# A gated recurrence: outputs moved to GpSimd, products left in PSUM, seven row places

## The chip, the cores and the metric

The kernel runs on one core of a Trainium2 chip. The metric is the time on the device in microseconds from the first to the last instruction with what lies around it, the median of the runs; lower is better. The core has a matrix engine (TensorE, "PE"), which writes to PSUM only; a vector engine (VectorE, "DVE"); an engine for activations (ScalarE, "ACT"); and GpSimd ("POOL"), which works on SBUF. Each follows its own queue in order and waits on semaphores.

## The reference, cut to what matters

One decoder layer on x of shape (2, 1024, 256): gated linear attention, a cross attention over 64 gathered context rows, and a block with self attention and 8 experts, a layer norm behind each. The change touches the first one alone:

```
q, k: (2, 1024, 16 heads, 8);  v: (2, 1024, 16, 16)
g = log_sigmoid(x @ Wgk1 @ Wgk2 + bgk2) / 16
h[t] = h[t-1] * exp(g[t])[..., None] + k[t][..., None] * v[t][..., None, :]   # scan over t
o[t] = einsum('bhk,bhkv->bhv', q[t] * 8**-0.5, h[t])
o = o * rsqrt(mean(o*o) + eps) * gnw * silu(x @ Wg);  x = layernorm(x + o @ Wo)
```

## The kernel before

The function `front` holds the whole of the first attention. The 128 partitions are 16 heads times 8 key channels; the free axis is the 1024 tokens of one batch. The 16 value columns of 2 batches make NJ = 32 steps jj. A step works on one row of 1024 values per partition:

- `values(jj)` on PE: 4 matmuls with a selection matrix spread value column jj over the key channels, into PSUM banks 2 (jj % 2) and the next, so two steps have places.
- `product(jj)` on DVE (L521): those banks times KT (the keys), into place jj % 6 of the SBUF tile `qh`.
- `state(jj)` on DVE (L526): the scan h = decay * h + product, in place in `qh`.
- `output(jj)` on DVE (L531): `qh` times QT (the queries), in place.
- `sums(q)` on PE (L314), for four steps at a time: matmuls with `headsum` add the 8 key channels of each head; then ACT copies the result (`OT`, L686), PE transposes it (`turn`, L320), ACT puts it into the token rows O (`tokens`, L689).

The semaphores s_v, s_kv, s_h, s_qh and s_s count the values, products, scans, outputs and sums that are done. `values(jj)` waits for product jj-2 (`s_kv`), and `product(jj)` for the sums that free its place of `qh`. On DVE the loop reads: scan jj; the extra work of this step if it is one of a first kind; product jj+1; output jj; the extra work if it is of a second kind.

The order of each queue is written out by hand. Extra work lies at fixed steps. Of the first kind on DVE: the rounding remainders of the value parts `parts_lo` (steps 2, 12, 19; L514) and of x `x_lo` (steps 4, 6; L505), `log_sigmoid` (11), `out_means` of block 0 (18), `out_rstd` (23, 28), which ends in the small operation called `nmr`. Of the second kind: `out_gated` (19, 21; L846 to L850, the result is the tile z), `out_means` of block 1 (20), `out_stats` (22, 27; L134 and L139), the key and value blocks of the cross attention (30; L602). On PE in step jj: `values(jj+2)`, then every fourth step `sums` and `turn`, in others the projections of the second batch, the gates, the transposes of z (19 and 25), the output products (L866 and L867; 21, 22, 26, 27), the matmuls of the context's keys (29, 30; L458 to L465), and `counts`, one-hot matmuls of the token lists. ACT makes the one-hot rows for them with 65 sign operations (`signs`, L696), spread over the steps, besides all the copies out of PSUM that are not on DVE. After the last step the ends of all these lead into the next block of the program, which PE, DVE and ACT enter together.

GpSimd sets constants and issues DMAs until 22 us, and then does nothing until the next block.

Of the kernel before, what the change touches and what calls it, by code (L numbers as in the profile page):

```python
# [16 lines left out]
ALU = mybir.AluOpType  # L17
# [44 lines left out]
class Kernel:  # L62
# [99 lines left out]
    def front(self, c):  # L162
# [8 lines left out]
        RQ, RS = 6, 6  # L171
# [52 lines left out]
        PASSES = ((0, 0), (1, 0), (0, 1))  # L224
        with nc.Block() as block:
# [10 lines left out]
            def _(e):  # L236
# [14 lines left out]
                for h in range(P // HD):  # L251
                    e.dma_start(gnw[h * HD:(h + 1) * HD, :], a["L0_attn_gnw"].rearrange("(p o) -> p o", o=1)).then_inc(s_wo, 16)
            @block.tensor
            def _(e):
# [41 lines left out]
                def values(jj):  # L296
                    n, j = jj // DK, jj % DK
                    if jj >= 2:
                        e.wait_ge(s_kv, jj - 1)
                    elif jj:  # L300
                        e.wait_ge(V.sem, V.at("k0"))
                    else:
                        e.wait_ge(self.C.sem, self.C.at(f"sel{DK - 1}"))
# [174 lines left out]
                e.wait_ge(s_kv, NJ)  # L478
# [15 lines left out]
            def _(e):  # L494
# [20 lines left out]
                def product(jj):  # L515
                    e.wait_ge(s_v, jj + 1)
                    if jj == HD:
                        e.wait_ge(A.sem, A.at("k1"))
                    if jj >= RQ:
                        e.wait_ge(s_s, (jj - RQ) // 4 + 1)  # L520
                    e.tensor_tensor(qh[:, jj % RQ, :], wide(2 * (jj % 2)), KT[:, batch(jj // HD)], ALU.mult).then_inc(s_kv, 1)  # L521
                def state(jj):
                    e.wait_ge(s_kv, jj + 1)
                    if jj % HD == 0:
                        e.wait_ge(A.sem, A.at(f"decay{jj // HD}"))
                    e.tensor_tensor_scan(qh[:, jj % RQ, :], decay[:, batch(jj // HD)], qh[:, jj % RQ, :], 0.0, ALU.mult, ALU.add).then_inc(s_h, 1)  # L526
                def output(jj):
                    e.wait_ge(s_h, jj + 1)
                    if jj % HD == 0:
                        e.wait_ge(A.sem, A.at(f"q{jj // HD}"))  # L530
                    e.tensor_tensor(qh[:, jj % RQ, :], qh[:, jj % RQ, :], QT[:, batch(jj // HD)], ALU.mult).then_inc(s_qh, 1)  # L531
# [32 lines left out]
                for jj in range(NJ):  # L564
                    state(jj)
                    if jj == 2:
# [17 lines left out]
                    if jj + 1 < NJ:  # L584
                        product(jj + 1)
                    output(jj)
# [2223 lines left out]
```

## Time and profile before

| | us |
|---|---|
| median of 3 runs (lowest, highest) | 1365.08 (1364.91, 1366.44) |
| the profiled execution: span of its instructions | 1364.6 |
| DVE busy in the whole span | 984.8 (72%) |
| PE busy in the whole span | 1288.8 (94%) |
| 32 scans, busy | 73.0 |
| 32 products, busy | 38.6 |
| 32 outputs, busy | 38.9 |
| 65 sign operations of ACT, busy | 70.7 |
| recurrence on DVE, first product to last output | 23.3 to 194.3 |

A row of a timeline is: start in us, duration in us, engine, line, operation, output tile <- input tiles, shapes, and in brackets the idle time of the engine just before it with what ended it. A duration runs from an instruction's start to its end; the next one of the same engine can start about 0.1 us before that end. A list of waits names the engine and line that waited, what it waited for, the sum in us, the number of times and the longest. A table of stretches gives for each engine the busy us and the instructions, and PEclk, the clock granted to TensorE as a share of 2.4 GHz; it is 0.5 at the engine's lower level of 1.2 GHz.

### The profile page before, as it was taken

How to read it: one execution, taken by the hardware profiler on the slowest of the kernel's cores; microseconds unless marked ns; L12 is line 12 of the kernel's file. 1: busy time of each engine (PE TensorE's matmuls, PEld its weight loads, DVE VectorE, ACT ScalarE, POOL GpSimd, SP SyncE). 2: the span in 40 equal slices, each digit the busy share in tenths (PEclk: the TensorE clock that was granted, in tenths of full speed). 3: DMA queues.
4: the chain of work that ended last, by engine and by line, in shares of the span. 5: the costliest groups of instructions: out<-in, count | busy, mean ns of one | idle time of the engine just before them, and what ended most of it. 6: DMA issues, size and time to landing. Idle time of an engine off the chain costs nothing.

```text
span 1364.6 us, 19112 instructions
## 1 busy us (share of the span) xinstructions
PE 1288.8 (94%) x7622; PEld 953.5 (70%) x7622; DVE 984.8 (72%) x1417; ACT 642.7 (47%) x942; POOL 139.4 (10%) x220
## 2 busy tenths in 40 slices
PE   8786868999899999999999999999999999999997
PEld 6453536667655555558888788888888888888886
DVE  7999997898799888848676655655646555555566
ACT  5787664346468877874433432322223223223233
POOL 5000003000524433310000000000000000000000
PEclk9898889999999999989999999999999999999999
DMA  5000001003612212203000011201101102010001
GB/s 140 1 1 0 0 1 35 1 1 133 200 49 70 60 52 55 59 29 109 16 1 16 16 55 41 72 21 39 47 9 47 39 16 70 16 39 16 0 16 47
DMA packets 40328, 55.78 MB, mean 41 GB/s; under 512 B 9552, under 2 KB 26624, under 8 KB 40240
## 3 DMA queue, kind: packets, MB, share of 16 engines
q1 hardware_dynamic: 35056, 43.67, 10.7%
q0 software_dynamic: 3648, 10.09, 2.5%
q8 instruction: 60, 0.98, 0.3%
q10 hardware_dynamic: 1536, 0.81, 0.2%
q14 instruction: 28, 0.23, 0.1%
HBM read 43.73 MB, written 10.55 MB: 40 GB/s over the span
## 4 chain that ended last, share of the span: by engine, by line
PE 52%; DVE 2%; ACT 0%; issue 0%; ACTq 0%; DVEq 0%
PE PS L2502 25%; PE PS L2515 24%; PE PS L2265 1%; PE PS L114 0%; PE PS L2528 0%; PE PS L2246 0%; PE PS L2279 0%; DVE OT_all L2663 0%; DVE r_st L2341 0%; DVE r_on L2358 0%; DVE r_on L2338 0%; PE PS L2540 0%; DVE X L2350 0%; DVE x_mid L2654 0%; ACT X L2624 0%
## 5 line engine op out<-in xcount | busy, mean ns | idle before, releaser
L2585 ACT ACTIVATE x_g<-PS,x_bias 128x512 f32<-128x512 f32 x256 | 175.8, 687 | 493.0 <-PE PS L2502 492.9
L2502 PE MATMUL PS<-x_h,x_w 128*128 128x512 f32 x1536 | 398.6, 395 | 0.0
L2515 PE MATMUL PS<-x_mid,x_w 128*128 128x512 f32 x1488 | 383.9, 393 | 1.1 <-DVE x_w L2237 1.1
L2502 PEld LDWEIGHTS PS<-x_h,x_w 128*128 128x128 f32 x1536 | 285.9, 188 | 64.7
L2515 PEld LDWEIGHTS PS<-x_mid,x_w 128*128 128x128 f32 x1488 | 279.6, 188 | 65.6 <-DVE x_w L2237 1.6
L2654 DVE CAST x_mid<-x_g 128x512 fp32r<-128x512 f32 x256 | 109.3, 427 | 268.0 <-ACT x_g L2585 267.7
L2104 DVE TENSOR_REDUCE a_M<-PS 128x2 f32<-128x1024 f32 (+1 forms) x144 | 173.1, 1223 | 24.6 <-PE PS L1801 18.5
L2656 DVE TENSOR_TENSOR x_mid<-x_g,x_mid 128x512 fp32r<-128x512 f32 x256 | 177.2, 692 | 8.8
L2042 ACT ACTIVATE f_parts<-PS 128x512 f32<-128x512 f32 x224 | 120.7, 601 | 36.5 <-PE PS L1855 24.9
L1878 PE MATMUL PS<-f_parts,aV 128*32 128x256 f32 (+1 forms) x960 | 75.1, 394 | 0.2 <-POOL f_parts L1689 0.2
L526 DVE TENSOR_TENSOR_SCAN qh<-decay,qh 128x1024 f32<-128x1024 f32 x32 | 73.0, 2282 | 0.0
L696 ACT ACTIVATE c_hot<-c_idxT,c_cid 128x1024 bf16<-128x1024 bf16 x65 | 70.7, 1140 | 3.5 <-PE PS L337 2.2
L2482 POOL DMA_DIRECT2D x_wb<-route_w x31 | 16.7, 539 | 476.3 <-DVE OT_all L2663 453.4
L1855 PE MATMUL PS<-aQ,aK 64*128 64x512 f32 x192 | 50.7, 485 | 0.5 <-ACT f_h L2042 0.5
L2663 DVE SCALAR_TENSOR_TENSOR OT_all<-PS,x_bias,x_wb 128x512 f32<-128x512 f32 x62 | 46.2, 745 | 0.0
L1855 PEld LDWEIGHTS PS<-aQ,aK 64*128 64x128 f32 x192 | 20.3, 183 | 37.0 <-ACT f_parts L2042 27.0
L1689 POOL TENSOR_SCALAR_AFFINE_SELECT f_parts<-f_parts 128x512 f32<-128x512 f32 x45 | 28.5, 634 | 162.2 <-ACT f_parts L2042 142.7
L307 PE MATMUL PS<-vparts,g_sel 128*128 128x512 f32 x128 | 39.3, 432 | 5.2 <-DVE qh L521 4.5
L1797 PE MATMUL PS<-aK,aQ 64*128 64x512 f32 (+3 forms) x256 | 36.3, 327 | 7.0 <-PEq L1058 2.7
L2237 DVE TENSOR_TENSOR x_w<-x_raw,x_w 128x1024 fp32r<-128x1024 f32 x32 | 39.4, 1233 | 2.0 <-ACT x_w L2232 2.0
L521 DVE TENSOR_TENSOR qh<-PS,KT 128x1024 f32<-128x1024 f32 x32 | 38.6, 1206 | 1.4 <-PE PS L314 1.3
L531 DVE TENSOR_TENSOR qh<-qh,QT 128x1024 f32<-128x1024 f32 x32 | 38.9, 1215 | 0.0
(383 smaller groups left out, 1593.9 us busy)
## 6 DMA issues: line engine op xcount, KB each, us to landing
x_raw<-L_ffn_e_w SPq DMA_DIRECT2D x32, 512.0 KB, 3.8
qk_parts<-f_parts SPq DMA_DIRECT2D x16, 512.0 KB, 3.3
x_wb<-route_w POOLq DMA_DIRECT2D x31, 256.0 KB, 3.4
aQ<-qk_parts SPq DMA_DIRECT2D x96, 64.0 KB, 2.5
aK<-qk_parts SPq DMA_DIRECT2D x60, 64.0 KB, 2.7
X<-x SPq DMA_DIRECT2D x4, 512.0 KB, 7.5
aK<-qk_parts SPq DMA_DIRECT2D x36, 48.0 KB, 2.0
out<-X SPq DMA_DIRECT2D x3, 512.0 KB, 2.9
```

The source lines that it names most:

```text
L526: e.tensor_tensor_scan(qh[:, jj % RQ, :], decay[:, batch(jj // HD)], qh[:, jj % RQ, :], 0.0, ALU.mult, ALU.add).then_inc(s_h, 1)
L696: e.activation(hot[:, n % RS, :], self.idxT[:, :], ACT.Sign, bias=self.cid[:, c:c + 1], scale=2.0).then_inc(s_sg, 1)
L1855: last = e.matmul(bank, K[q][R, s, tile(TB * h if kind == "k0" else kind)], Q[q][R, s, q0:q0 + BLK], start=True, stop=True)
L1878: last = e.matmul(PS[32 * j:32 * j + 32, 7, dst:dst + w], Vs[m % 2][:, kt, j, :], x, start=k in (0, 3) and half == 0, stop=k in (2, NQD - ...
L2042: e.activation(buf[k][:, j, :], PS[:, 4 + b % 3, :], ACT.Exp).then_inc(A.sem, 1)
L2104: e.tensor_reduce(dst, src, AX.X, ALU.max, negate=True).then_inc(VC.sem, 1)
L2502: last = e.matmul(PS[:, f % 2, :], w1[n % 2][u][:, kt, f * P:(f + 1) * P], self.rows(v, k)[:, kt, :], start=m == 0 and kt == 0, stop=m == ...
L2515: last = e.matmul(PS[:, 2 + 2 * (it % 2) + d, :], w2[n % 2][v][:, f, d * P:(d + 1) * P], mid[u][:, f % RM, :], start=f == 0 and m == 0, st ...
L2585: e.activation(g[s % RG][:, :], PS[:, f % 2, :], ACT.Gelu, bias=b1[:, n, f:f + 1]).then_inc(A.sem, 1)
L2654: e.tensor_copy(mid[0][:, f % RM, :], g[s % RG][:, :]).then_inc(V.sem, 1)
L2656: e.tensor_tensor(mid[1][:, f % RM, :], g[s % RG][:, :], mid[0][:, f % RM, :].bitcast(F32), ALU.subtract).then_inc(V.sem, 1)
L2663: e.scalar_tensor_tensor(out=(y if n else sumT[k])[:, d, :], in0=PS[:, 2 + 2 * (it % 2) + d, :], scalar=b2[:, n, d:d + 1], in1=wb[:, it % ...
```

## The change

GpSimd takes the outputs of steps 0 to 30, in order, behind its constants; the last one stays on DVE. The product is written back into the PSUM banks in which the values stand, and the scan reads it there and writes to `qh`. So `values(jj)` waits for scan jj-2 in place of product jj-2, and the wait for a free place of `qh` moves from the product to the scan. `qh` has seven places instead of six. On DVE product jj+1 now follows scan jj directly, ahead of the extra work of both kinds. At the end of the queue PE's transposes of x, which overwrite bank 0, wait for 31 scans instead of 32 products.

```diff
-        RQ, RS = 6, 6
+        RQ, RS = 7, 6
...
             @block.gpsimd
...
+                for jj in range(NJ - 1):
+                    output(e, jj)
...
                 def values(jj):
...
-                        e.wait_ge(s_kv, jj - 1)
+                        e.wait_ge(s_h, jj - 1)
...
-                e.wait_ge(s_kv, NJ)
+                e.wait_ge(s_h, NJ - 1)
                 self.c_turn(e, 0)
...
-                    if jj >= RQ:
-                        e.wait_ge(s_s, (jj - RQ) // 4 + 1)
-                    e.tensor_tensor(qh[:, jj % RQ, :], wide(2 * (jj % 2)), KT[:, batch(jj // HD)], ALU.mult).then_inc(s_kv, 1)
+                    e.tensor_tensor(wide(2 * (jj % 2)), wide(2 * (jj % 2)), KT[:, batch(jj // HD)], ALU.mult).then_inc(s_kv, 1)
                 def state(jj):
                     e.wait_ge(s_kv, jj + 1)
                     if jj % HD == 0:
                         e.wait_ge(A.sem, A.at(f"decay{jj // HD}"))
-                    e.tensor_tensor_scan(qh[:, jj % RQ, :], decay[:, batch(jj // HD)], qh[:, jj % RQ, :], 0.0, ALU.mult, ALU.add).then_inc(s_h, 1)
-                def output(jj):
...
+                    if jj >= RQ:
+                        e.wait_ge(s_s, (jj - RQ) // 4 + 1)
+                    e.tensor_tensor_scan(qh[:, jj % RQ, :], decay[:, batch(jj // HD)], wide(2 * (jj % 2)), 0.0, ALU.mult, ALU.add).then_inc(s_h, 1)
...
                 for jj in range(NJ):
                     state(jj)
+                    if jj + 1 < NJ:
+                        product(jj + 1)
+                    else:
+                        output(e, jj)
                     if jj == 2:
                         parts_lo(1)
...
-                    if jj + 1 < NJ:
-                        product(jj + 1)
-                    output(jj)
                     if jj == 19:
                         self.out_gated(e, 0)
```

## Rows read from the trace of the kernel before

**Rows 1.** Busy time by stretch: us, PE, PEld, DVE, ACT, POOL, PEclk, DMA share, GB/s

```profile
124.00:147.00 23.00, 16.35 (x92) 10.72 (x96) 22.86 (x20) 14.95 (x16) 0.00 (x0) 0.85 0.00 1
```

**Rows 2.** Timeline of DVE: output, scan and product of neighbouring steps

```profile
108.09 1.21 DVE L531 TENSOR_TENSOR qh<-qh,QT 128x1024 f32<-128x1024 f32 x1
109.22 2.28 DVE L526 TENSOR_TENSOR_SCAN qh<-decay,qh 128x1024 f32<-128x1024 f32 x1
111.43 1.20 DVE L521 TENSOR_TENSOR qh<-PS,KT 128x1024 f32<-128x1024 f32 x1
```

**Rows 3.** Timeline of DVE: the first product and the first scan

```profile
23.31 1.22 DVE L521 TENSOR_TENSOR qh<-PS,KT 128x1024 f32<-128x1024 f32 x1
24.57 2.29 DVE L526 TENSOR_TENSOR_SCAN qh<-decay,qh 128x1024 f32<-128x1024 f32 x1
```

**Rows 4.** Waits of DVE, 24 to 195 us: sum in us, times, longest

```profile
DVE XTp L505 <- ACT XTp L651: 2.6, 1, 2.6
DVE qh L521 <- PE PS L314: 1.3, 1, 1.3
DVE vparts L514 <- ACT vparts L681: 1.3, 2, 0.9
```

**Rows 5.** Waits of PE for DVE, 59.5 to 122 us

```profile
PE PS L263 <- DVE XTp L505: 1.4, 1, 1.4
PE PS L314 <- DVE vparts L514: 0.7, 1, 0.7
```

**Rows 6.** Timeline of DVE: `parts_lo` of step 19, the gating of block 0, scan 20

```profile
122.64 1.23 DVE L514 TENSOR_TENSOR vparts<-PS,vparts 128x1024 fp32r<-128x1024 f32 x1 [0.92 <-ACT vparts L681]
...
126.04 0.55 DVE L846 RECIPROCAL go_rs<-go_rs 128x64 f32<-128x64 f32 x1
...
129.02 2.28 DVE L526 TENSOR_TENSOR_SCAN qh<-decay,qh 128x1024 f32<-128x1024 f32 x1
```

**Rows 7.** Timeline of ACT: the square roots of blocks 0 and 1

```profile
123.92 0.35 ACT L841 ACTIVATE go_rs<-go_ms,eps 128x64 f32<-128x64 f32 x1
...
138.68 0.31 ACT L841 ACTIVATE go_rs<-go_ms,eps 128x64 f32<-128x64 f32 x1
```

**Rows 8.** Timeline of PE, 129 to 198 us

```profile
129.25 1.94 PE L114 MATMUL PS<-ident,z 128*128 128x128 f32 x8 [6.77 <-DVE z L850]
...
142.27 1.20 PE L307 MATMUL PS<-vparts,g_sel 128*128 128x512 f32 x4
...
145.46 0.59 PE L867 MATMUL PS<-X,ident 128*128 128x256 f32 x2
...
152.05 2.07 PE L307 MATMUL PS<-vparts,g_sel 128*128 128x512 f32 x4 [4.52 <-DVE qh L521]
...
177.24 3.62 PE L314 MATMUL PS<-qh,headsum 128*32 128x512 f32 x16 [5.60 <-ACT X L886]
...
186.42 1.03 PE L465 MATMUL PS<-decay,c_L 128*128 128x256 f32 x4
...
195.56 1.92 PE L314 MATMUL PS<-qh,headsum 128*32 128x512 f32 x16
```

**Rows 9.** Timeline of DVE: statistics of blocks 0 and 1, key blocks, scan 31

```profile
146.47 1.42 DVE L134 BATCH_NORM_STATS2 go_st<-PS 128x6 f32<-128x256 f32 x4
...
170.84 1.42 DVE L134 BATCH_NORM_STATS2 go_st<-PS 128x6 f32<-128x256 f32 x4
...
187.73 2.48 DVE L602 TENSOR_TENSOR c_Kblk<-PS,c_m 128x512 f32<-128x512 f32 x4
...
190.79 2.28 DVE L526 TENSOR_TENSOR_SCAN qh<-decay,qh 128x1024 f32<-128x1024 f32 x1
```

**Rows 10.** Timeline of POOL, 11 to 18 us

```profile
11.78 1.16 POOL L943 TENSOR_SCALAR_AFFINE_SELECT c_selaug<-c_selaug 128x1024 fp32r<-128x1024 f32 x1
...
13.77 2.84 POOL L943 TENSOR_SCALAR_AFFINE_SELECT c_selaug<-c_selaug 128x256 fp32r<-128x256 f32 x3
17.11 0.42 POOL L943 TENSOR_SCALAR_AFFINE_SELECT c_selaug<-c_selaug 128x256 fp32r<-128x256 f32 x1 [0.50 <-POOL c_selaug L943]
```

More of the change, by code:

```diff
@@ L224, in front, with output @@
         PASSES = ((0, 0), (1, 0), (0, 1))
+        def output(e, jj):
+            e.wait_ge(s_h, jj + 1)
+            if jj % HD == 0:
+                e.wait_ge(A.sem, A.at(f"q{jj // HD}"))
+            e.tensor_tensor(qh[:, jj % RQ, :], qh[:, jj % RQ, :], QT[:, batch(jj // HD)], ALU.mult).then_inc(s_qh, 1)
         with nc.Block() as block:
@@ L525, in state @@
                         e.wait_ge(A.sem, A.at(f"decay{jj // HD}"))
-                    e.tensor_tensor_scan(qh[:, jj % RQ, :], decay[:, batch(jj // HD)], qh[:, jj % RQ, :], 0.0, ALU.mult, ALU.add).then_inc(s_h, 1)
-                def output(jj):
[L528 to L531, printed above, removed]
+                    if jj >= RQ:
+                        e.wait_ge(s_s, (jj - RQ) // 4 + 1)
+                    e.tensor_tensor_scan(qh[:, jj % RQ, :], decay[:, batch(jj // HD)], wide(2 * (jj % 2)), 0.0, ALU.mult, ALU.add).then_inc(s_h, 1)
                 e.wait_ge(A.sem, A.at("wl"))
```

## The prediction

> **What bounds the kernel now.** I read the busy time by stretch first, since the change touches only the recurrence (23 to 194 us of the profiled execution). There DVE is busy nearly all the time, 22.86 of 23 us in the stretch from 124, PE and ACT much less [rows 1]. Next its own order: a step is scan, product, output, and the starts lie 1.13 us apart from output to scan and 2.21 from scan to product; with 1.11 from product to output (1.20 long, less the overlap of 0.09 that the output shows too) a step is 4.45 us [rows 2]. A scan that follows its own product directly, as the first one does, starts 1.26 us after it, so 0.13 later than one with work in between [rows 3]. So taking 31 outputs from DVE looks like 31 x 1.13 = 35.0 us. But the list of what DVE waited for has three entries in the recurrence: x_lo 2.6, a product 1.3, parts_lo 1.3 (two times) [rows 4]. They are short, and they are the places to look at: at each, DVE had caught up with a chain on PE and ACT, and a faster DVE only waits longer there. What PE waited for between 59.5 and 122 us settles it: on DVE only 1.4 us once and 0.7 us once, each right behind one of those same two DVE operations [rows 5]. Between them PE and ACT ran at their own pace. The reader should see two lists with almost equal lengths, not one busy engine and two idle ones.
>
> **Part 1, up to the gating of block 0: about 2 us gained.** The x_lo of step 6, the parts_lo of step 12 and the parts_lo of step 19 each ended an idle time of DVE, behind ACT copies that hang on PE. They can't start earlier, so the 6, 12 and 19 outputs ahead of them buy nothing. What is gained is what stood between the joint and the next scan: the product moves ahead of it and the output goes. At the third joint parts_lo starts at 122.64 and gating at 126.04 [rows 6]; two operations go, 1.11 + 1.13 us [rows 2], but gating then meets ACT's square root, which ended at 124.27 and, by my estimate, ends 0.3 earlier now [rows 7]. I put gating at 124.0, scan 20 at 127.0 instead of 129.02, 2.0 earlier. The seventh row place is costed at nothing here: the buffer wait behind it is the 1.3 us product wait of rows 4 late in the recurrence, and the waits of part 2 lie over it.
>
> **Part 2, the new hand-over.** Before, the selection matmuls of step j+2 (`values`) waited for product j; now they wait for scan j, since the scan reads the bank. From then DVE has product j+1 and scan j+1, 1.26 + 2.20 = 3.5 us, until it wants product j+2. Queued behind this wait on PE is everything of step j+2 and later: sums, transposes, output products. PE's matmuls for one step take 1.20 us and the sums of four steps 1.92 [rows 8], so two or three steps in four carry more than 3.5 us of PE work, and the rest waits. Leg by leg, with the durations of before:
> - From the transposes of z (129.25) through ACT to the square root of block 1 (138.68) 9.43 us pass on PE and ACT [rows 7, 8]. From 127.25 that gives 136.7, its end 137.0. Gating takes 129.02 - 126.04 = 2.98 [rows 6], scan 22 runs from 140.0 to 142.3, and only then may `values(24)` go. From its start (142.27) to the end of the output product behind it (145.46 + 0.59) are 3.8 us [rows 8]: 146.1. The statistics of block 0 start at 146.2 instead of 146.47 [rows 9]. The 2 us are down to 0.3.
> - From the statistics to scan 23 I take 1.9 us, 1.42 for their first part [rows 9] and an estimate of 0.4 for the small second. Scan 23 starts at 148.05, scan 24 2.20 + 1.26 later at 151.5, ends at 153.8; `values(26)` starts at 153.85, where before it started at 152.05, behind product 24 [rows 8]. Now 1.8 us late.
> - From `values(26)` to the statistics of block 1 (170.84) 18.8 us pass on PE with waits on ACT alone [rows 8, 9]: 172.65, 1.8 late.
> - From there to the sums of group 6 (177.24) 6.4 us pass over the statistics, scan 28, the small `nmr` operation, ACT's row copies [rows 8, 9]. Product 29 now stands ahead of `nmr`, 1.13 more: 180.2, 2.95 late.
> - PE and ACT take it from there to the matmuls of the keys (186.42 + 1.03 = 187.45) [rows 8], now 190.4. The key blocks on DVE started at 187.73 [rows 9], 0.28 after; now at once, 190.4. So they, scan 31 (190.79 before, 193.5 now) and all behind them are **2.7 us later**.
>
> **Part 3, what the clock gives back.** The granted clock was 0.85 in the stretch from 124 us [rows 1]: PE fell to its 1.2 GHz level in the long waits (6.77, 4.52 and 5.60 us), and the matmuls right behind them ran at it. At that level `values` took 2.07 instead of 1.20 us, the sums 3.62 instead of 1.92 [rows 8], so a low spell that catches both costs 2.6 us, and two of them (152 and 177 us) 5.1. The new order splits these gaps: the one ahead of `values(26)` is cut by `values(25)`, the one ahead of the sums by `values(30)`. If they vanish, the sum is 2.7 - 5.1 = -2.4; if a third one is added, by the new wait of `values(24)`, 2.7 + 2.6 = +5.3. I take a relief of 1.0, since a gap of over 4 us stays ahead of `values(25)` (146.1 to 150.4) and of `values(30)`. Sum: +2.7 - 1.0 = **+1.7 us**.
>
> **Operations the trace doesn't show.** A product that writes PSUM, and a scan that reads it: the nearest rows are a PSUM-read product at 1.20 us and an SBUF-only output at 1.22 [rows 2]. Bounds: 0.1 faster to 1.2 slower (a second pass). Only two products and three scans lie on the path above, so -0.2 to +3; DVE's new slack (31 us of idle) hides the others. I take 0, nearest in kind. The output on GpSimd: the nearest row is a one-input operation of the same size, 1.16 us [rows 10]; a second input makes 1.2 to 2.3. Next to DVE work the same small operation took 2.84/3 = 0.95 us instead of 0.42 [rows 10], so the upper bound is 2.3 x 2.25 = 5.2 us. I take 2.3. The new mean step is (193.5 - 24.6)/31 = 5.4 us, and a group's sums come behind a `values` that waits for the next scan, so anything up to 5.2 us is covered and costs nothing. GpSimd's queue is free by 23 us; its next work stands in the next block. That cover is gone above 5.4 us. The last output stays on DVE, 1.2 us as before.
>
> The long pieces of 0.95 us lay beside DVE operations on SBUF operands. The Trainium skill (SBUF — State Buffer, "Who interferes with whom") says a DVE instruction with two SBUF inputs contends with a GpSimd instruction that reads SBUF, one with a single SBUF input doesn't; the trace of before agrees as far as those rows go and can't show the second half. The skill's GPSIMD Engine Reference (section 3.1) also speaks against moving two-input work there, about 2.6 cycles per element; at its 1.2 GHz an estimate from that page is 2.2 us, and the sum would be the same.
>
> **The rivals.**
> A. DVE alone is the bound and PE keeps up: -31 x 1.13 - 1.3 + 32 x 0.13 = -32 us, 1333. For it: DVE's busy share [rows 1]. Against: rows 4 and 5. Chance 0.05. A weaker form, in which the late legs are loose and only the joints of part 1 hold, gives back the 11 outputs after scan 20, -2 - 11 x 1.13, less 3 = about -11, 1354: 0.10.
> B. The legs hold, and PE stays at 2.4 GHz because its gaps are split: -2.4, 1362.7. Chance 0.17, half of it faster than the bound.
> C. The legs hold, and the wait of `values(24)` and `values(25)` adds a low spell: +5.3, 1370.4. Chance 0.13. Slower side; it decides once PE idles in front of step 22 as long as it did ahead of the slow matmuls of rows 8.
> D. GpSimd becomes the bound: from 5.4 us per output on. At 6 us the last of 31 ends at 26.9 + 186 = 213, and the last sums, at 195.6 before [rows 8], wait for it: +17, 1382. It needs the SBUF contention also with the scans. Chance 0.05. A product of twice the length, with DVE as the bound again, about 1372: 0.02.
> Forecast, legs as worked out, clock about as before: 0.48.
>
> **How the numbers follow.** The span of 1364.6 us lies 0.5 below the median of 1365.08; the sum is a difference and goes onto the median: 1365.1 + 1.7 = 1366.8. What a measurement can tell from no change is 0.2%, 2.7 us: faster is under 1362.4, slower above 1367.8. The forecast's own spread (1.5 us either way, ACT's 65 one-hot operations shifting against PE) puts two thirds of 0.48 inside, a third above. Faster: 0.15 + 0.08 = 0.23. Same: 0.31 + 0.09 = 0.40. Slower: 0.17 + 0.13 + 0.07 = 0.37. The range leaves out both forms of A, D and the double product, 0.22 in all: 1359 to 1371.5. The forecast's own range is 1363 to 1370.
>
> **What the profile after would show.** DVE's busy time in the recurrence 31 outputs (37.8 us) lower while its end hardly moves; DVE idle ahead of products, released by the `values` matmuls, of x_lo and parts_lo, and of the statistics, released by the output products, some 30 us in all. x_lo still at 58 to 59 us, parts_lo at 88 and 122 to 123. PE waiting on scans ahead of `values(24)` to `values(26)`. Scans and products within 0.1 us of before. GpSimd at 2 to 2.5 us an output, mostly idle. Wrong if DVE shows no such waits (A), if PE waits for GpSimd (D), or if the statistics of block 1 start before 168 us: then leg 3 fails.

## The result and the profile after

| | before | after |
|---|---|---|
| median of 19 runs each on one chip (lowest, highest), us | 1365.4 (1363.7, 1369.2) | 1368.64 (1364.9, 1370.9) |
| ratio after to before, 95% interval | | 1.0019 [1.0012, 1.0026] |
| span of the profiled execution, us | 1364.6 | 1367.8 |
| DVE busy in the whole span, us | 984.8 | 955.3 |

The change takes 31 outputs from DVE, and the kernel is slower by 0.19%, 2.6 us by the ratio (3.2 by the medians). The interval excludes no change, but the loss is only about the 0.2% that the prediction took as the least that a measurement can tell. The runs of one kernel spread over some 6 us (1364.9 to 1370.9 for after), and each kernel has one trace, of one execution: after's took 0.9 us more than its median. So verdicts go by medians and ratios, and traces are read for where the time goes.

The costliest groups of the page of after that the change touches (line, engine, operation, tiles, shapes, count | busy us, mean ns | idle before, releaser):

```profile
L229 POOL TENSOR_TENSOR qh<-qh,QT 128x1024 f32<-128x1024 f32 x31 | 73.7, 2377 | 89.5 <-DVE qh L534 89.5
L534 DVE TENSOR_TENSOR_SCAN qh<-decay,PS 128x1024 f32<-128x1024 f32 x32 | 73.0, 2281 | 0.6
L527 DVE TENSOR_TENSOR PS<-PS,KT 128x1024 f32<-128x1024 f32 x32 | 38.9, 1217 | 18.4 <-PE PS L315 18.3
```

All three unknown operations are as costed: an output on GpSimd takes 2.38 us (2.3 taken), and the product and scan over PSUM last as long as in [rows 2]. GpSimd waits for a scan ahead of every output, and no engine's list of waits names it. The scans wait 0.6 us in all, so the seventh place of `qh` is enough; it was not priced alone. Now DVE's list of waits, 24 to 195 us, which answers [rows 4]:

```profile
DVE PS L527 <- PE PS L315: 18.3, 11, 5.3
DVE go_st L134 <- PE PS L871: 8.3, 2, 5.5
DVE XTp L513 <- ACT XTp L655: 3.1, 2, 2.6
DVE vparts L522 <- ACT vparts L685: 2.4, 3, 1.6
DVE go_rs L850 <- ACT go_rs L845: 2.2, 2, 1.8
```

5.2 us of waits have become 38 (with three small ones not shown, 3.5 us together): the freed time has turned into waiting for PE's `values` (L315), for the output products (L871) and for ACT. The end of the recurrence didn't come nearer. Leg by leg, from the two timelines (start in us):

| | before | after, forecast | after, measured | difference |
|---|---|---|---|---|
| `x_lo` of step 6 | 58.59 | not earlier | 55.60 | -3.0 |
| scan 20 | 129.02 | 127.0 | 124.15 | -4.9 |
| scan 22 | 142.03 | 140.0 | 137.69 | -4.3 |
| statistics of block 0 | 146.47 | 146.2 | 143.84 | -2.6 |
| scan 24 | 153.05 | 151.5 | 150.35 | -2.7 |
| `values(26)` | 152.05 | 153.85 | 152.68 | +0.6 |
| statistics of block 1 | 170.84 | 172.65 | 171.01 | +0.2 |
| sums of group 6 | 177.24 | 180.2 | 179.61 | +2.4 |
| key blocks on DVE | 187.73 | 190.4 | 191.22 | +3.5 |
| scan 31 | 190.79 | 193.5 | 194.29 | +3.5 |

PE after, 124 to 191 us, which answers [rows 8]: the new waits are the ones released by `DVE qh L534`, the scans.

```profile
124.38 1.94 PE L114 MATMUL PS<-ident,z 128*128 128x128 f32 x8 [5.06 <-DVE z L854]
...
140.02 1.19 PE L315 MATMUL PS<-vparts,g_sel 128*128 128x512 f32 x4 [2.01 <-DVE qh L534]
...
143.21 0.59 PE L871 MATMUL PS<-X,ident 128*128 128x256 f32 x2
148.01 2.07 PE L315 MATMUL PS<-vparts,g_sel 128*128 128x512 f32 x4 [4.21 <-DVE qh L534]
...
152.68 2.08 PE L315 MATMUL PS<-vparts,g_sel 128*128 128x512 f32 x4 [1.62 <-DVE qh L534]
...
175.18 2.07 PE L315 MATMUL PS<-vparts,g_sel 128*128 128x512 f32 x4 [4.21 <-DVE qh L534]
179.61 3.64 PE L322 MATMUL PS<-qh,headsum 128*32 128x512 f32 x16 [2.36 <-ACT X L890]
184.40 1.97 PE L328 MATMUL PS<-ident,OT 128*128 128x128 f32 x8 [1.15 <-ACT OT L690]
```

`values(24)` waits 2.01 us for scan 22, and the output products that stand behind it on PE, which the statistics of block 0 need, wait with it. The statistics are at 143.84, when 143.21 + 0.59 has ended. DVE had nothing to do from 141.1 on. In all PE waits 12.3 us for scans in the recurrence, in five places.

One row was not foreseen. The small operation `nmr`, 0.16 us before, in both blocks (DVE, then GpSimd, then ACT after):

```profile
175.04 1.21 DVE L527 TENSOR_TENSOR PS<-PS,KT 128x1024 f32<-128x1024 f32 x1
176.16 0.17 DVE L148 RECIPROCAL go_rstd<-go_sd 128x4 f32<-128x4 f32 x1
176.36 1.23 DVE L884 SCALAR_TENSOR_TENSOR go_nmr<-go_mv,go_rstd 128x4 f32<-128x4 f32 x1
```

```profile
175.20 2.36 POOL L229 TENSOR_TENSOR qh<-qh,QT 128x1024 f32<-128x1024 f32 x1 [8.41 <-DVE qh L534]
```

```profile
177.62 1.93 ACT L890 ACTIVATE X<-PS,go_nmr,go_rstd 128x256 f32<-128x256 f32 x4 [2.26 <-DVE go_nmr L884]
```

`nmr` works on 4 values per partition and ends at 177.59, just when GpSimd's output ends (175.20 + 2.36 = 177.56). The row copies and the sums of group 6 stand behind it.

### The profile page after: what moved, and what is told of

It reads as the page before. It is cut to its first block, busy times and chain, and to the rows that moved or that the text cites. A ratio compares the mean times of both kernels' runs of the same rounds, so it can differ in the third digit from the quotient of the medians.

```text
span 1367.8 us, 19111 instructions
## 1 busy us (share of the span) xinstructions
PE 1290.3 (94%) x7622; PEld 953.9 (70%) x7622; DVE 955.3 (70%) x1386; ACT 642.9 (47%) x942; POOL 213.7 (16%) x251
## 4 chain that ended last, share of the span: by engine, by line
PE 52%; DVE 2%; ACT 0%; issue 0%; ACTq 0%; DVEq 0%
PE PS L2506 25%; PE PS L2519 24%; PE PS L2269 1%; PE PS L114 0%; PE PS L2532 0%; PE PS L2250 0%; PE PS L2283 0%; DVE OT_all L2667 0%; DVE r_st L2345 0%; DVE r_on L2362 0%; DVE r_on L2342 0%; PE PS L2544 0%; DVE X L2354 0%; DVE x_mid L2658 0%; ACT X L2628 0%
## 5 line engine op out<-in xcount | busy, mean ns | idle before, releaser
L229 POOL TENSOR_TENSOR qh<-qh,QT 128x1024 f32<-128x1024 f32 x31 | 73.7, 2377 | 89.5 <-DVE qh L534 89.5
L534 DVE TENSOR_TENSOR_SCAN qh<-decay,PS 128x1024 f32<-128x1024 f32 x32 | 73.0, 2281 | 0.6
L315 PE MATMUL PS<-vparts,g_sel 128*128 128x512 f32 x128 | 41.8, 453 | 13.1 <-DVE qh L534 12.3
L527 DVE TENSOR_TENSOR PS<-PS,KT 128x1024 f32<-128x1024 f32 x32 | 38.9, 1217 | 18.4 <-PE PS L315 18.3
L315 PEld LDWEIGHTS PS<-vparts,g_sel 128*128 128x128 f32 x128 | 24.4, 210 | 26.4 <-DVE qh L534 16.6
```

## Experiments

All ratios are to the kernel before on the same chip at the same time, 95% intervals in brackets. Kernels of different times are compared by their ratios; 0.1% is 1.37 us. The places in us are from one traced execution each, and these lie differently to their medians: those of `a_gwait`, `a_nmr1`, `a_noout` and `b_noout` took 3.2, 2.6, 1.9 and 1.2 us less than the median, those of `a_order2` and `b_order` 2.8 and 1.0 more. The kernel after and `a_gwait` do the same work up to scan 19 and start that scan at 115.60 and 113.92 us.

### Outputs left out of the kernel before, and of the kernel after

Both leave out 31 output products (so the sums add the states, not the states times the queries). `b_noout` keeps the old hand-over, `a_noout` the new one.

```diff
 b_noout
-                    output(jj)
+                    if jj == NJ - 1:
+                        output(jj)
 a_noout
-                for jj in range(NJ - 1):
-                    output(e, jj)
 both
-                    e.wait_ge(s_qh, 4 * q + 4)
+                    e.wait_ge(s_h, 4 * q + 4)
+                    if q == NQ - 1:
+                        e.wait_ge(s_qh, 1)
```

> The kernel before, with the 31 outputs of steps 0 to 30 left out on every engine (the sums read the states themselves); product, hand-over and order as before. It asks what DVE's 35.0 us of outputs are worth without the new wait. Two-lists theory (PE and ACT bind at the joints): 3 to 7 us faster than before, about 1360.5; x_lo, parts_lo still wait for ACT, parts_lo of step 19 at 119 to 121 us; values(26) at about 147.5, as it still waits for a product. DVE-is-the-bound rival: 30 to 35 us faster, about 1332, no new idle time on DVE.

> The kernel after, with its 31 outputs on GpSimd left out (the sums read the states); product in PSUM and the new hand-over kept. Two-lists theory: GpSimd is not on the path but for the two small nmr operations that read two SBUF operands (1.23 us instead of 0.16), so 2 us faster than after, about 1366.5, and about as slow as before. GpSimd rival (the outputs on GpSimd slow DVE or delay the sums): 5 us or more faster than after, 1363 or less.

`b_noout`: 1362.9 us, 0.9986 [0.9976, 0.9995], less than the 3 to 7 us of the theory; the rival (30 to 35) is far off. This is what taking the outputs off DVE brings in this order with nothing put in their place: 1.9 us of the 35 that stood on DVE. In the trace scan 20 is at 124.22, 4.8 earlier than before, and the key blocks at 182.91, still 4.8 earlier. So the whole gain comes by scan 20, as in after, and 3.0 of it stand at the `x_lo` of step 6 already (55.58 against 58.59); the later outputs buy nothing.

`a_noout`: 1365.4 us, 1.0006 [0.9996, 1.0016], 1.8 us by the ratio ahead of after, as the theory had it. Scan 20 at 122.42, the key blocks at 186.34. From scan 20 on it loses 5.2 us against `b_noout` (63.92 against 58.69 us): the new hand-over, together with the new order on DVE, which the two kernels also differ in. Over the whole, by the ratios, it is 2.7 us. The operation `nmr` is short again without GpSimd beside it:

```profile
147.40 0.17 DVE L148 RECIPROCAL go_rstd<-go_sd 128x4 f32<-128x4 f32 x1
147.60 0.16 DVE L884 SCALAR_TENSOR_TENSOR go_nmr<-go_mv,go_rstd 128x4 f32<-128x4 f32 x1
```

### One SBUF input for nmr

The mean is left out: `nmr` is minus the root alone, so that it reads one SBUF tile instead of two.

```diff
+        if m < 2:
+            e.tensor_scalar(self.o_nmr[m % 2][:, :], self.o_rstd[m % 2][:, :], -1.0, None, ALU.mult).then_inc(self.OV[m].sem, 1)
+            return
```

> The kernel after, with the two nmr operations of blocks 0 and 1 in a form with one SBUF tensor input (the mean is left out of them, so these blocks' normalisation lacks it). Port theory (a DVE operation with two SBUF inputs waits until GpSimd's running output ends): nmr at 0.15 to 0.2 us instead of 1.23, both on the path, 2 us faster, 1366.5. Rival (nmr is long because it follows the reciprocal or the product closely): nmr stays at 1.2 us and the time at 1368.6.

1368.9 us, 1.0028 [1.0017, 1.0039]: nothing gained, and the row says why.

```profile
173.54 1.21 DVE L527 TENSOR_TENSOR PS<-PS,KT 128x1024 f32<-128x1024 f32 x1
174.65 0.17 DVE L148 RECIPROCAL go_rstd<-go_sd 128x4 f32<-128x4 f32 x1
174.85 1.23 DVE L885 TENSOR_SCALAR go_nmr<-go_rstd 128x4 f32<-128x4 f32 x1
```

GpSimd's output ran from 173.70 to 176.07, `nmr` ended at 176.08: it waited as before. The numbers are the rival's, but its cause is not: in `a_noout` (above) and `a_gwait` (below) `nmr` follows the reciprocal just as closely, without GpSimd beside it, and takes 0.16. A theory that counts inputs alone is wrong, and the prediction gave the page's rule without its condition when it wrote that an instruction with a single SBUF input doesn't contend. The reciprocal beside it, one SBUF input too, did not wait (0.17). The Trainium skill (SBUF — State Buffer, "Who interferes with whom") has the missing half: besides instructions with two SBUF inputs, a `tensor_scalar` from SBUF to SBUF can take the shared pair of ports in one of its two-port modes. The trace agrees: 1.23 us, ended with GpSimd's output to 0.01. No run here has this `tensor_scalar` without GpSimd beside it (the form with two inputs takes 0.16 then), and why the reciprocal stays out no run here tests.

### GpSimd held back at two steps

```diff
                 for jj in range(NJ - 1):
+                    if jj == 23:
+                        e.wait_ge(self.OV[0].sem, self.OV[0].at("nmr"))
+                    elif jj == 28:
+                        e.wait_ge(self.OV[1].sem, self.OV[1].at("nmr"))
                     output(e, jj)
```

> The kernel after, where GpSimd starts the outputs of steps 23 and 28 only once the small operation nmr of block 0 and of block 1 has ended; nothing else differs, nothing is left out. Theory: nmr took 1.23 instead of 0.16 us because it wants the SBUF port that GpSimd holds for its output; with GpSimd held back nmr is 0.16 again in both blocks, the row copies and the sums of group 6 are 1.1 us earlier, and the ratio to before falls from 1.0019 by 0.001 to 0.002, to 1.000 to 1.001; the two outputs start about 0.3 to 0.5 us later than before and nobody waits for them. It is read from the medians and from nmr's row. Rival (GpSimd's price in the medians, 3 us against the kernel with its outputs left out, is not these two waits but the clock or other waits): nmr shortens and the ratio stays at 1.0015 to 1.0025.

1366.4 us, 1.0010 [0.9999, 1.0020]. It falls by 0.0009, about the least that the theory had, and the interval overlaps that of after, so the verdict rests on the trace. DVE and then GpSimd:

```profile
174.23 0.16 DVE L888 SCALAR_TENSOR_TENSOR go_nmr<-go_mv,go_rstd 128x4 f32<-128x4 f32 x1
```

```profile
174.48 4.67 POOL L229 TENSOR_TENSOR qh<-qh,QT 128x1024 f32<-128x1024 f32 x2 [9.78 <-DVE go_nmr L888]
```

From the statistics of block 1 to the sums of group 6 pass 176.42 - 168.88 = 7.54 us, against 8.60 in after: 1.06 less, the length of the port wait. (My fourth leg had 6.40 + 1.13 = 7.53.) The kernel is level with `a_noout` (1.0010 and 1.0006, each to 0.001), so nothing of a price of GpSimd is left that these runs can measure.

### The old hand-over with GpSimd, and the new one with DVE's outputs

`a_sbuf` is the kernel after with the product in SBUF again and `values` behind the product. `b_psum` is the kernel before with the product left in PSUM, `values` behind the scan and seven places of `qh`. In both the wait for a free place moves along, to the operation that writes `qh` first (cut from the lines below). Nothing is left out of either.

```diff
 a_sbuf
-                        e.wait_ge(s_h, jj - 1)
+                        e.wait_ge(s_kv, jj - 1)
...
-                    e.tensor_tensor(wide(2 * (jj % 2)), wide(2 * (jj % 2)), KT[:, batch(jj // HD)], ALU.mult).then_inc(s_kv, 1)
+                    e.tensor_tensor(qh[:, jj % RQ, :], wide(2 * (jj % 2)), KT[:, batch(jj // HD)], ALU.mult).then_inc(s_kv, 1)
...
-                    e.tensor_tensor_scan(qh[:, jj % RQ, :], decay[:, batch(jj // HD)], wide(2 * (jj % 2)), 0.0, ALU.mult, ALU.add).then_inc(s_h, 1)
+                    e.tensor_tensor_scan(qh[:, jj % RQ, :], decay[:, batch(jj // HD)], qh[:, jj % RQ, :], 0.0, ALU.mult, ALU.add).then_inc(s_h, 1)
 b_psum
-        RQ, RS = 6, 6
+        RQ, RS = 7, 6
...
-                        e.wait_ge(s_kv, jj - 1)
+                        e.wait_ge(s_h, jj - 1)
...
-                    e.tensor_tensor(qh[:, jj % RQ, :], wide(2 * (jj % 2)), KT[:, batch(jj // HD)], ALU.mult).then_inc(s_kv, 1)
+                    e.tensor_tensor(wide(2 * (jj % 2)), wide(2 * (jj % 2)), KT[:, batch(jj // HD)], ALU.mult).then_inc(s_kv, 1)
...
-                    e.tensor_tensor_scan(qh[:, jj % RQ, :], decay[:, batch(jj // HD)], qh[:, jj % RQ, :], 0.0, ALU.mult, ALU.add).then_inc(s_h, 1)
+                    e.tensor_tensor_scan(qh[:, jj % RQ, :], decay[:, batch(jj // HD)], wide(2 * (jj % 2)), 0.0, ALU.mult, ALU.add).then_inc(s_h, 1)
```

> The kernel after with the product written to SBUF (qh) as before and the old hand-over (values waits for the product), outputs on GpSimd. Port theory: the scan now has two SBUF inputs and waits for GpSimd's output of the step before, so a step is 2.4 + 2.3 + 0.1 = 4.8 us where nothing else waits, scan rows of 3 us and more, and the whole is 3 to 10 us slower than before, about 1372. Rival (no contention, the new hand-over alone cost the gain): scans stay 2.28 us and the time is that of the kernel before without outputs, 4 to 5 us faster than before, about 1361.

> The kernel before with the product left in PSUM, the scan reading it there, `values` behind scan j-2 and seven row places; all 32 outputs stay on DVE, in the old order. Nothing is left out. It prices the new hand-over with the old DVE load. With 31 outputs left out, the new hand-over together with the new order cost 2.4 us in the medians (1362.9 against 1365.4), since a `values` behind scan j then has 3.5 us of DVE work to hide in. Theory (the wait costs what DVE's queue no longer covers): here an output of 1.1 us stands in that stretch too, 4.6 us, so the PE work of most steps fits and `values` is late only at steps with sums; ratio to before 1.000 to 1.0015, PE waiting on scans ahead of the same `values` (25 and 26) for 2 to 4 us. Rival (the hand-over costs a fixed 3.5 us or more wherever it stands, through the low-clock matmuls that its waits bring): 1.0025 or above. Second rival (the seventh place and the free wait ahead of the scan instead of the product matter): below 0.999.

`a_sbuf`: 1369.5 us, 1.0029 [1.0017, 1.0041], 4.0 us slower than before by the ratio, within the theory's 3 to 10; the rival (faster than before) fell. Its scans, first the group and then two of them with the product between:

```profile
L534 DVE TENSOR_TENSOR_SCAN qh<-decay,qh 128x1024 f32<-128x1024 f32 x32 | 92.9, 2903 | 0.6
```

```profile
94.90 3.43 DVE L534 TENSOR_TENSOR_SCAN qh<-decay,qh 128x1024 f32<-128x1024 f32 x1
98.25 1.19 DVE L529 TENSOR_TENSOR qh<-PS,KT 128x1024 f32<-128x1024 f32 x1
99.48 3.48 DVE L534 TENSOR_TENSOR_SCAN qh<-decay,qh 128x1024 f32<-128x1024 f32 x1
```

17 of 32 scans take 3.3 to 3.5 us instead of 2.28. The output on GpSimd starts when a scan ends (98.41), the product has no second SBUF input and runs beside it in 1.19 us, the next scan (decay and `qh`, both SBUF) starts at 99.48 and ends 2.15 us after the output's end at 100.81. So it stands still until GpSimd has finished. A plain step is 99.48 - 94.90 = 4.58 us; with the outputs on DVE it was 4.45. Here the rule can be laid beside rows: the Trainium skill (SBUF — State Buffer, "Who interferes with whom") says that a DVE instruction with two SBUF inputs contends with a GpSimd instruction that reads SBUF, and one with a single SBUF input outside the two-port modes doesn't; the trace agrees, after has 2.28 us for a scan that reads its product from PSUM, `a_sbuf` 3.48. So leaving the product in PSUM is what keeps the scans short beside GpSimd. It doesn't pay for the new hand-over, though: after is only 0.0010 ahead of `a_sbuf`, 1.4 us, and the two intervals overlap.

`b_psum`: 1372.0 us, 1.0053 [1.0040, 1.0067]. The theory (0 to 0.15%) fell, its rival held. PE's waits for scans in this kernel, and the place where output products stand behind one:

```profile
PE PS L307 <- DVE qh L526: 19.9, 12, 4.2
```

```profile
148.58 1.20 PE L307 MATMUL PS<-vparts,g_sel 128*128 128x512 f32 x4 [2.01 <-DVE qh L526]
...
151.78 0.59 PE L867 MATMUL PS<-X,ident 128*128 128x256 f32 x2
156.58 2.08 PE L307 MATMUL PS<-vparts,g_sel 128*128 128x512 f32 x4 [4.21 <-DVE qh L526]
```

The statistics of block 0 start at 152.41, 5.9 us later than before, those of block 1 at 179.36, 8.5 later; the key blocks at 195.73, 8.0 later. My error was to look at the free time behind a step's `values`. What counts is what `values` now holds up on PE. From scan 20 on that is the output products with the statistics behind them. But scan 20 itself is at 132.99, 4.0 later than before: half of the loss arises where PE's waits hold up gates, sums and projections (7.7 of the 19.9 us lie before 128 us). That DVE, still full, can make up for nothing afterwards fits both halves, but no run tests it. So the hand-over alone costs 7.2 us by the ratio; with the outputs gone and the new order on DVE, 2.7 (`a_noout` against `b_noout`). The outputs alone bring 1.9. The two parts don't add: 7.2 - 1.9 = 5.3 us, and both together measured 0.8 (`a_noout`).

### The order behind the new wait

`a_pe` puts PE's output products ahead of the `values` of their step. `a_order2` has this, `out_rstd` ahead of the product as in the kernel before, and GpSimd held back as above. `b_order` is the kernel before with PE's move alone. Nothing is left out. The lines taken out at the old places, and those that hold GpSimd back, are cut here.

```diff
                 for jj in range(NJ):
+                    if jj == 22:
+                        self.out_product(e, 0, SB, (2, 3))
+                    elif jj == 27:
+                        self.out_product(e, 1, SB, (2, 3))
                     if jj + 2 < NJ:
                         values(jj + 2)
...
                     state(jj)
+                    if jj == 23:
+                        self.out_rstd(e, 0)
+                    elif jj == 28:
+                        self.out_rstd(e, 1)
                     if jj + 1 < NJ:
                         product(jj + 1)
```

> The kernel after with three places reordered, nothing left out: PE's output products of token tiles 2 and 3 of both blocks (steps 22 and 27) stand ahead of the `values` of their step instead of behind it, `out_rstd` with nmr stands ahead of the product again, as in the kernel before, and GpSimd holds back the outputs 23 and 28 until nmr has ended. Theory (the new wait costs because the output products are queued behind it on PE, and the statistics, the root and the sums of group 6 hang on them): the statistics of block 0 start at 141.1 instead of 143.8 in the profiled execution, those of block 1 about 4 us earlier than 171.0, the sums of group 6 5 to 6 us earlier than 179.6, and the whole is 3 to 6 us faster than the kernel after, ratio to before 0.9975 to 0.9995. Rival (the legs are set by the scans of DVE, or what is gained is lost in later waits at the keys and the last sums): statistics earlier, the start of scan 31 less than 1.5 us earlier, and a ratio of 1.001 to 1.002.

> The kernel before with the same move on PE alone: the output products of tiles 2 and 3 of both blocks ahead of the `values` of their step. Nothing is left out. Before, this `values` waited for nothing there, so the move buys only its length, 1.2 us at each of two places, and product 24 (or 29) may come later by 2.6 us, which DVE's queue (scan 23 and the root in between) hides. Theory: 0.5 to 2 us faster, ratio 0.9985 to 0.9997, so less than the same move brings the kernel after; if so, the changed kernel with it is about level with or ahead of this one. Rival (the order of PE is worth as much here, 3 to 6 us): 0.9955 to 0.998, and the change then is not what should be kept.

> The kernel after with PE's move alone: output products of tiles 2 and 3 of both blocks ahead of the `values` of their step; `out_rstd` stays behind the product and GpSimd holds nothing back. Nothing is left out. It divides the 5.9 us between the kernel with only GpSimd held back (1366.4) and the one with all three moves (1360.5). Theory (the queue position of the output products behind the new wait is the main cost): statistics at 141 and 167 us, nmr 1.23 us in both blocks, and 1363.0 to 1364.5, ratio 0.9985 to 0.9998; the order of `out_rstd` and the port wait are then worth 2.5 to 4 us together. Rival (the gain comes from `out_rstd` ahead of the product): 1365.5 or more, ratio above 1.0003.

| | median | ratio | statistics 0 | statistics 1 | sums 6 | key blocks |
|---|---|---|---|---|---|---|
| after | 1368.6 | 1.0019 | 143.84 | 171.01 | 179.61 | 191.22 |
| `a_gwait` | 1366.4 | 1.0010 | 142.24 | 168.88 | 176.42 | 186.25 |
| `a_pe` | 1365.0 | 0.9998 [0.9989, 1.0006] | 141.08 | 168.02 | 176.62 | 186.62 |
| `a_order2` | 1360.5 | 0.9969 [0.9957, 0.9980] | 140.46 | 165.86 | 172.27 | 182.51 |
| `b_order` | 1364.0 | 0.9992 [0.9982, 1.0002] | 146.76 | 171.12 | 177.53 | 187.96 |

DVE in `a_order2`: the statistics follow the product without a gap, and the small operations stand ahead of the next product.

```profile
139.34 1.21 DVE L531 TENSOR_TENSOR PS<-PS,KT 128x1024 f32<-128x1024 f32 x1
140.46 1.41 DVE L134 BATCH_NORM_STATS2 go_st<-PS 128x6 f32<-128x256 f32 x4
...
165.86 1.42 DVE L134 BATCH_NORM_STATS2 go_st<-PS 128x6 f32<-128x256 f32 x4 [4.58 <-PE PS L875]
...
170.08 0.16 DVE L888 SCALAR_TENSOR_TENSOR go_nmr<-go_mv,go_rstd 128x4 f32<-128x4 f32 x1
170.16 1.23 DVE L531 TENSOR_TENSOR PS<-PS,KT 128x1024 f32<-128x1024 f32 x1
```

`a_order2` is the fastest full kernel: 0.31% ahead of before and 0.50%, 6.8 us, ahead of after, somewhat more than the 3 to 6 expected, though its trace is of one of its slower executions. PE's order alone is worth 2.9 us of that (`a_pe` against after), `out_rstd` and the held-back GpSimd together 4.0. `a_pe` lies just above its expected 1363.0 to 1364.5. The statistics of block 0 come 2.8 us earlier than in after, as the table shows; in the column of `a_gwait` 1.7 of its distance from after stand at scan 19 already and have nothing to do with the change. The same move on PE brings the kernel before 1.1 us by the ratio, as expected; the interval goes from 2.5 us to none. There `values(24)` waits for a product that is long done, and there is little to overtake. `a_order2` and `b_order` have intervals that don't overlap, so the changed kernel in its best order beats the old one with the same move. The loss of after is mainly one of order: its queues were written for a `values` that hardly ever waits.

### What hangs on ACT

`a2_thin` (from `a_order2`) and `b_thin` (from before) let the 65 one-hot operations of ACT cover 64 of 1024 columns, so only part of the tokens is counted; six fills on DVE ahead of the recurrence set the other columns once. `a2_dsign` moves these operations to DVE, two or three a step, with the weights of the window doubled, and leaves nothing out.

```diff
 a2_thin, b_thin
-    e.activation(hot[:, n % RS, :], self.idxT[:, :], ACT.Sign
+    e.activation(hot[:, n % RS, 0:64], self.idxT[:, 0:64], ACT.Sign
...
 a2_dsign, on DVE in place of ACT's
+    e.tensor_scalar(hot[:, n % RS, :], self.idxT[:, :], float(c), 0.5, ALU.is_ge, ALU.subtract).then_inc(s_sg, 1)
```

> The reordered kernel (all three moves) where the 65 one-hot operations of ACT cover 64 of 1024 columns, the rest of these rows being constants set once; so the counts of the tokens are not the reference's. It takes some 60 of 70.7 us from ACT and leaves PE, DVE and GpSimd the same instructions. It asks how much of the time hangs on ACT now. Theory (the chains through ACT are bound by their own copies, and what is left is the exchange between DVE's scans and PE): only the 3.1 us wait of PE for the last one-hot rows at 186 us and small delays of copies go: 2 to 5 us faster than the reordered kernel, 1355.5 to 1358.5, ratio 0.993 to 0.9955. Rival (ACT is the engine that sets the joints): more than 8 us faster, ratio below 0.991. Against both (no cover is lost by ACT's load at all): 0 to 1 us.

> The kernel before where ACT's 65 one-hot operations cover 64 of 1024 columns, the rest of these rows being constants; the counts of the tokens are not the reference's. The same cut made the reordered kernel 8 us faster (1352.5 against 1360.5). It asks whether ACT's relief is worth as much with DVE as full as it was before the change. Theory (before, DVE's own list of about 4.45 us a step and the chains through ACT and PE were almost equally long, so relief on either alone buys little, and the change together with the reordering opens DVE's side): 1 to 4 us faster than before, ratio 0.997 to 0.9993, DVE's idle time gone and scan 31 at 187 to 190 us. Rival (ACT alone set the joints before too): 7 us or more, ratio below 0.995.

> The reordered kernel with the 65 one-hot operations on DVE instead of ACT, two or three per step behind the product and the extra work, as a comparison less 0.5, with window weights of plus and minus 1.0; the same counts come out, nothing is left out. DVE has some 35 us of idle time in the recurrence. Each is an operation with one SBUF input and an SBUF output, of the kind that waited for GpSimd's output when nmr was rewritten that way (1.23 us beside it against 0.16 alone). Theory (it waits for GpSimd's port, and GpSimd then waits for it): an operation is 0.3 to 0.6 us where GpSimd is idle, and the first one behind each product waits for about 1.2 us; 31 such waits and 65 x 0.45 = 29 us make 60 to 70 us on DVE, 25 to 35 more than its idle time: 15 to 40 us slower than the reordered kernel, ratio above 1.008. Rival (bf16 operations of that kind don't wait, or DVE hides them in waits for PE): within 3 us of the reordered kernel or faster, as far as the thin version shows room, ratio 0.993 to 0.999.

`a2_thin`: 1352.5 us, 0.9906 [0.9889, 0.9923], 8.0 us (by the ratios 8.6) faster than `a_order2`: beyond the theory's numbers and at the rival's bound (more than 8), so ACT's load sets much of what is left, more than the wait for the last one-hot rows that I had counted. `b_thin`: 1364.9 us, 0.9998 [0.9988, 1.0008], so nothing, less than either text had. DVE's waits in `b_thin`, 24 to 195 us:

```profile
DVE XTp L505 <- ACT XTp L653: 2.5, 1, 2.5
DVE qh L521 <- PE PS L314: 1.3, 1, 1.3
DVE go_rs L848 <- ACT go_rs L843: 0.7, 1, 0.7
```

With ACT relieved DVE waits about as little as in [rows 4] and takes as long: scan 31 at 191.15. Before, relieving ACT alone brought nothing and relieving DVE alone 1.9 us; with DVE relieved and the queues in order, ACT's relief brings 8. That fits two lists of equal length. It is not the whole proof: ACT relieved with DVE relieved but without the new hand-over and order was not run.

`a2_dsign`: 1407.6 us, 1.0308 [1.0294, 1.0322], slower than even the theory said. The group (busy, mean, idle before it):

```profile
L546 DVE TENSOR_SCALAR c_hot<-c_idxT 128x1024 bf16<-128x1024 bf16 x65 | 45.9, 742 | 30.9 <-PE PS L347 27.5 <-PE PS L349 3.4
```

```profile
65.08 1.72 DVE L546 TENSOR_SCALAR c_hot<-c_idxT 128x1024 bf16<-128x1024 bf16 x1
69.45 0.43 DVE L546 TENSOR_SCALAR c_hot<-c_idxT 128x1024 bf16<-128x1024 bf16 x1 [2.65 <-PE PS L347]
```

Alone it takes 0.43 us, beside GpSimd (an output from 64.12 to 66.52) 1.72: the port wait is there. But 45.9 us are only 15 more than the 31.1 that DVE waited in `a_order2`. What is new is that DVE waits 30.9 us until PE's counts free one of the six one-hot rows, while PE's counts stand behind `values` that wait for DVE's scans. 45.9 + 30.9 = 76.8, less the other waits of DVE, which fall by 28.9 us, from 31.1 to 2.2 in the recurrence, gives 47.9 us, and the kernel is 47 slower than `a_order2`. The theory had the sign and the port, not this circle.

## Why the prediction was right, and where only its sum was

The forecast was +1.7 us, the measurement +2.6 by the ratio and +3.2 by the medians. The mechanism held; several terms did not, and they cancelled, so that the sum came this close is in part luck. By the prediction's own bounds the median of 1368.6 lies among the slower (above 1367.8, chance 0.37), while its forecast and its largest chance (0.40) lay on "same".

Sorted by kind, as an estimate from the rows below: up to the key blocks the clock gave back 1.4 us (2.8 at 37 and 47 us, less some 1.4 later: 0.5 in leg 1 and 1.3 in leg 5, with 0.4 won in leg 3) where 1.0 was taken, and the legs without it came to 3.5 + 1.4 = 4.9 us where 2.7 was taken. Nearly all of these 2.2 us are the two waits of `nmr` for GpSimd, which the sum had at nothing.

**The bound: right.** DVE's busy time from 24 to 197 us fell by 33 us (not 37.8: an output takes 1.13 from start to start, and the long `nmr` counts as busy), and the end of the recurrence moved 3.5 us the other way. `b_noout` gives it in one number: 1.9 us for 31 outputs. `b_thin` adds the second list: nothing for ACT's relief. Rival A (1333) and its weak form (1354) fell.

**Part 1: mis-sized, -4.9 instead of -2.0.** The third joint gave 1.7 us (from `parts_lo` to scan 20 pass 4.65 us instead of 6.38), close to the 2.0 taken. The failed sentence is that the joints "can't start earlier": `x_lo` of step 6 came 3.0 earlier, and with it `parts_lo` at 84.98 and 119.50 in place of "88 and 122 to 123". The 2.9 us arose ahead of the joint of step 6, on PE, at the clock. PE after, then before, each with the row of the stretch from 24 to 59 us, whose third number from the end is the clock:

```profile
24.00:59.00 35.00, 27.82 (x177) 19.24 (x176) 30.40 (x20) 22.83 (x23) 16.69 (x7) 1.00 0.00 1
...
36.94 3.14 PE L291 MATMUL PS<-Wgp,XTp 128*128 128x256 f32 x24 [1.46 <-DVE vparts L522]
...
45.44 1.92 PE L322 MATMUL PS<-qh,headsum 128*32 128x512 f32 x16 [1.67 <-DVE XTp L513]
```

```profile
24.00:59.00 35.00, 28.14 (x167) 20.16 (x165) 32.30 (x23) 19.83 (x20) 0.00 (x0) 0.90 0.00 0
...
37.11 4.63 PE L283 MATMUL PS<-Wgp,XTp 128*128 128x256 f32 x24 [1.77 <-DVE vparts L514]
...
47.13 3.25 PE L314 MATMUL PS<-qh,headsum 128*32 128x512 f32 x16 [2.27 <-DVE XTp L505]
```

1.49 us less for the gates and 1.33 for the sums: behind slightly shorter waits PE kept its 2.4 GHz (granted clock 1.00 from 24 to 59 us, 0.90 before). This is no accident of one trace. The gates took 4.63 or 4.64 us in the three traces in which the wait ahead of them was 1.77 us (before, `b_order`, `b_thin`) and in `a_sbuf` (3.12), and 3.13 or 3.14 in the other ten (0.80 to 1.53). For the sums the wait just ahead doesn't decide alone: `b_noout` has 1.92 us behind 2.22, before 3.25 behind 2.27, and differs in the gates. My clock relief was looked for only in part 2. A chain's length is no constant when the waits inside it change.

**Part 2: leg by leg.** The square root of block 1 came 9.98 us after the transposes of z (9.43 taken), the statistics of block 0 3.82 after `values(24)` (3.8), scan 23 1.86 behind them (1.9). Then scan 24 came 4.65 us after scan 23 (3.46 taken): I had left out `out_rstd` in this leg. It costs 0.1 by itself (3.56 in `a_gwait`) and 1.1 for its port wait. Leg 3 was 18.33 us (18.8). Leg 4 was 8.60 (7.53): product 29 ahead of `nmr` as worked out, plus 1.07 for the port. Leg 5 was 191.22 - 179.61 = 11.6 (10.2): the turn at 1.97 instead of 1.09 us and the counts at 1.04 instead of 0.62. The sum of the misses is -2.9 + 0.55 + 1.2 - 0.5 + 1.1 + 1.4 = +0.85, so the key blocks came at +3.5 instead of +2.7. The waits that I named, of `values(24)` to `values(26)`, are there (2.01, 4.21 and 1.62), and that of `values(30)` (4.21) too.

**Part 3: wrong place, and late the wrong sign.** The granted clock after, 171 to 197 and 197 to 209 us:

```profile
171.00:197.00 26.00, 14.62 (x71) 6.52 (x72) 18.98 (x24) 15.38 (x20) 7.08 (x3) 0.68 0.00 0
197.00:209.00 12.00, 10.85 (x59) 7.98 (x59) 9.71 (x12) 8.27 (x8) 0.00 (x0) 0.83 0.00 1
```

Before it was 0.80 and 1.00. The relief of 1.0 came, and more, but at 37 us; toward the end the clock was lower than before, and `values(25)` and `values(30)` took 2.07 us behind the new waits, which is rival C's mechanism. Not every low spell comes in each execution: `values` and the sums at 64 us took 1.92 and 2.78 us in after, 1.19 and 1.92 in `a_gwait`, and nothing ahead of them differs between these two kernels. Over the whole recurrence (24 to 197 us) the clock is 0.88 after and 0.89 before, so "about as before" holds in the mean and nowhere in particular.

**Unknown operations: right by size, but I took only the size.** The bound for contention came from two small pieces of [rows 10] and was put on GpSimd's own instruction, where it cost nothing; rival D fell. This is the term of the sum that was put at nothing without a reason: contention in fact hit DVE, at an operation of 0.16 us on the path, and was worth 1.1 us per place. I had the rule on two SBUF inputs in the text and didn't go through DVE's operations with it; `nmr` has two.

## What to carry to other kernels

When work leaves an engine, ask first which waits it already ends: two short lists of waits on the two sides (here 5.2 us on DVE) mean that neither engine alone is worth relieving. When a change makes one operation wait longer, list what is queued behind it and move the urgent part ahead of it; that was worth 2.9 us here, and with the rest of the reordering (6.8 us in all) the kernel beats before and after. And when GpSimd gets SBUF work, go through every DVE operation that can run beside it, the tiny ones on the critical path above all.

## What the hardware showed that I had not expected

- A DVE operation on 128x4 values took 1.23 us instead of 0.16 beside a GpSimd instruction, and ended with it, to 0.03 us. Two forms did this, one with two SBUF inputs and a `tensor_scalar` with one; a reciprocal with one SBUF input (0.17 us) and products that read PSUM (1.21) did not.
- Where DVE came second, DVE waited: GpSimd's outputs stayed at 2.34 to 2.41 us in after and `a_sbuf`, also where DVE's scans went from 2.28 to 3.48. No run here has GpSimd coming second to a scan with two SBUF inputs.
- Shortening PE's waits at 37 and 47 us by 0.3 and 0.6 us went with matmuls that took 2.8 us less in sum.
